# Layer 0's B rows by broadcast transfers instead of bf16 split and select matmuls, and a second PSUM bank for the preparation

## The reference

```python
x_dbl = u @ w_xproj
delta = softplus(x_dbl[..., :DT_RANK] @ w_dt + b_dt)
Bm, Cm = x_dbl[..., DT_RANK:DT_RANK+16], x_dbl[..., DT_RANK+16:]
def step(h, inp):                       # over the 256 tokens
    d_t, b_t, c_t, u_t = inp
    dA = exp(d_t[..., None] * A)
    h = dA * h + (d_t * u_t)[..., None] * b_t[:, None, :]
    return h, einsum('bdn,bn->bd', h, c_t)
```

## Time and profile before

| | |
|---|---|
| median of runs | 2923.34 us |
| profiled execution | 2917.5 us, its span 2916.2 us |
| layer 0 (load to the end of its last sum) | to about 985 us of the span |
| full turns (t = 2 to 14) | 53.3 us each |
| of a full turn's 53 us | PE busy 47.27, DVE 49.44, ACT 28.60, POOL 23.03 us |
| granted TensorE clock | mean 0.945 over the span |

### The profile page before, as it was taken

One profiled execution on the slowest core, in us unless ns is written; L12 is line 12 of the kernel. 1 busy time (PEld: TensorE's weight loads), 2 busy tenths in 40 slices (PEclk: granted clock), 3 DMA queues, 4 the chain that ended last, 5 costly groups with the idle time before them and its releaser, 6 DMA issues.

```text
span 2916.2 us, 47757 instructions
## 1 busy us (share of the span) xinstructions
PE 2373.6 (81%) x18201; PEld 1678.6 (58%) x18201; DVE 2152.4 (74%) x4587; ACT 1433.4 (49%) x3688; POOL 839.7 (29%) x453
## 2 busy tenths in 40 slices
PE   4788889889887757888888888858999976676776
PEld 2456666666665654666666666635666654454544
DVE  3389999999988443767676767645666626999997
ACT  0355555555555114676767676613434334555553
POOL 0044344344444301222222222200000002555444
PEclk9999999999998877999999999969999998999988
DMA  1011110111111450000000000010110003445442
GB/s 63 16 38 38 45 45 30 45 45 41 42 37 52 148 180 1 1 1 2 1 2 1 1 1 1 1 38 20 29 29 8 6 25 117 159 146 167 145 169 95
DMA packets 71348, 147.97 MB, mean 51 GB/s; under 512 B 6864, under 2 KB 37072, under 8 KB 70608
## 3 DMA queue, kind: packets, MB, share of 16 engines
q1 hardware_dynamic: 69072, 140.73, 14.5%
q0 software_dynamic: 2048, 4.20, 0.4%
HBM read 135.20 MB, written 9.18 MB: 50 GB/s over the span
## 4 chain that ended last, share of the span: by engine, by line
PE 48%; DVE 21%; issue 12%; POOL 9%; ACT 7%; DMA 2%; SPq 0%; POOLq 0%; DVEq 0%; ACTq 0%
POOL h L2125 6%; PE psum L831 4%; PE psum L651 4%; DVE mx L1392 4%; DVE h L1514 3%; PE psum L647 3%; PE psum L389 2%; PE psum L699 2%; PE psum L538 2%; ACT pt L1880 2%; DVE h L1505 2%; PE psum L658 2%; PE psum L583 2%; PE psum L780 2%; PE psum L416 2%
## 5 line engine op out<-in xcount | busy, mean ns | idle before, releaser
L2091 POOL TENSOR_TENSOR h<-h,Crep 128x1024 f32<-128x1024 f32 x128 | 371.6, 2915 | 609.2 <-DVE h L1514 609.2
L2073 POOL TENSOR_TENSOR pr<-pr,rsum 128x512 f32<-128x512 f32 x192 | 202.2, 1057 | 643.9 <-DVE rsum L1358 642.2
L1514 DVE TENSOR_TENSOR_SCAN h<-dA,h 128x1024 f32<-128x1024 f32 x128 | 292.1, 2304 | 3.9 <-DVE h L1505 0.5
L1392 DVE TENSOR_REDUCE mx<-psum 128x4 f32<-128x1024 f32 (+1 forms) x192 | 226.5, 1215 | 80.0 <-PE psum L656 80.0
L2125 POOL TENSOR_TENSOR h<-h,Crep 128x1024 f32<-128x1024 f32 x64 | 196.4, 3068 | 243.3 <-DVE h L1268 243.3
L1880 ACT ACTIVATE pt<-psum 128x1024 f32<-128x1024 f32 x192 | 186.9, 1017 | 128.0 <-PE psum L658 128.0
L831 PE MATMUL psum<-h,pack_wf 128*128 128x256 f32 x1024 | 243.1, 392 | 5.4 <-POOL h L2091 5.4
L831 PEld LDWEIGHTS psum<-h,pack_wf 128*128 128x128 f32 x1024 | 199.9, 199 | 34.7 <-POOL h L2091 6.4
L1836 ACT ACTIVATE pr<-psum,nb 128x256 f32<-128x256 f32 (+1 forms) x512 | 210.5, 432 | 15.8 <-DVE nb L1350 15.8
L1977 ACT ACTIVATE dA<-delta,A 128x255 f32<-128x255 f32 x512 | 211.4, 495 | 13.1 <-DVE h L1514 11.7
L1846 ACT ACTIVATE prT<-psum 128x512 f32<-128x512 f32 x192 | 115.7, 603 | 163.1 <-PE psum L552 162.4
(11 more groups left out here) (342 smaller groups left out, 5426.9 us busy)
## 6 DMA issues: line engine op xcount, KB each, us to landing
Crep<-c_rows SPq DMA_DIRECT2D x64, 512.0 KB, 3.9
Brep<-bc_rows SPq DMA_DIRECT2D x64, 512.0 KB, 6.5
Crep<-bc_rows SPq DMA_DIRECT2D x64, 512.0 KB, 5.9
w1r<-m_w SPq DMA_DIRECT2D x32, 256.0 KB, 5.8
w2r<-m_w SPq DMA_DIRECT2D x32, 256.0 KB, 5.5
pack_wf<-wf SPq DMA_DIRECT2D x1, 3192.0 KB, 12.5
slots<-zero SPq DMA_DIRECT2D x12, 256.0 KB, 3.0
w1s<-s_w SPq DMA_DIRECT2D x8, 256.0 KB, 2.8
```

The lines of the kernel that those rows point to most:

```text
L1392: ve.e.tensor_reduce(mx[:, qb, 2 * h:2 * h + 2, groups[0]:groups[-1] + 1], k.psum[:, base:base + 2, :].rearrange("p i (n x) -> p i n x", n ...
L1514: ve.e.tensor_tensor_scan(flat(h), flat(k.dA[c][g % 2]), flat(h), 0.0, ALU.mult, ALU.add).then_inc(*k.set("scanned", 0, b, g, c))
L2091: po.e.tensor_tensor(h[:, :, :], h[:, :, :], k.Crep[n % 3][:, :, :], ALU.mult).then_inc(*k.set("hC", 0, b, g, c))
```

## The change

B takes the way that C had. `crow` (32 rows, B and C) is stored whole to DRAM, and `sp_b_spread` reads four B rows back, repeated for all partitions, into one of two Brep tiles in SBUF. The product reads Brep there, whole groups at a time (128x1024, one instruction for each c), and the scan of c waits for its own product alone. The bf16 split on DVE, the select matmuls on PE, the `selb` matrix and its cast are gone; empty steps stand in the table where the split was. Bank 6, which held the spread rows, becomes the second bank of the preparation: its steps alternate between banks 5 and 6, with a wait of their own where the single bank had implied one. The SP queue carries 64 more transfers of 512 KB.

```diff
+def pe_take0(k, s):
+
+    if k.pre0_read[s] is not None:
+        k.pe.wait_ge(*k.at(*k.pre0_read[s]))
+    return k.bank[s]
...
     yield
-    bk = pe_take(k, 0)
+    bk = pe_take0(k, 6)
+    pe.wait_ge(*k.at("xnT", 0, b))
     pe.e.matmul(bk[0:E0, 0:L], w["gate_w"], xnT[:, :], start=True, stop=True).then_inc(*k.set("gate", b))
-    k.pre_read = ("gz", b)
+    k.pre0_read[6] = ("gz", b)
     yield
-    bk = pe_take(k, 0)
+    bk = pe_take0(k, 5)
...
-        pe.e.matmul(bk[0:96, 0:L], w["w_bc"][:, c, :], u[:, c, :], start=c == 0, stop=c == CI - 1)
+        pe.e.matmul(bk[0:32, 0:L], w["w_bc"][:, c, :], u[:, c, :], start=c == 0, stop=c == CI - 1)
...
-def pe_spread(k, b, g, j):
...
-        i = pe.e.matmul(SB[:, m * L:(m + 1) * L], w["sel"][:, g * NG + 2 * j + m, :], k.split[b % 2][:, :], start=True, stop=True)
...
-    ve.e.tensor_copy(k.crow[b % 2][:, :], bk[0:32, 0:L]).then_inc(*k.set("crow", b))
-    yield
-    if b >= 2:
-        ve.wait_ge(*k.at("spread", 0, b - 2, 3, "B", 1))
-    ve.e.tensor_copy(split[:, :], bk[0:96, 0:L]).then_inc(*ve.step())
-    yield from rest(ve)
-    ve.e.tensor_tensor(k.sr[:, :], bk[0:64, 0:L], split[0:64, :], ALU.subtract).then_inc(*k.set("bc_read", b))
-    yield
-    ve.wait_ge(*k.at("bc_read", b))
-    ve.e.tensor_copy(split[0:64, :], k.sr[:, :]).then_inc(*ve.step())
-    yield from rest(ve)
-    ve.e.tensor_tensor(split[0:32, :], k.sr[0:32, :], split[0:32, :], ALU.subtract).then_inc(*k.set("split", 0, b))
+    ve.e.tensor_copy(k.crow[b % 2][:, :], b6[0:32, 0:L]).then_inc(*k.set("crow", b))
+    yield
+    yield
+    yield
+    yield
...
-def ve_product(k, b, g, j):
-    ve, SB = k.ve, k.bank[SPREAD_BANK]
+def ve_product(k, b, g, c):
+    ve, n = k.ve, 4 * b + g
     was = (b, g - 2) if g >= 2 else (b - 1, g + 2) if b else None
     ve.wait_ge(*k.at("dtu", b))
-    ve.wait_ge(*k.at("spread", 0, b, g, "B", j))
-    for c in range(CI):
-        if was is not None:
-            ve.wait_ge(*k.at("summed", 0, *was, c))
-        i = ve.e.tensor_tensor(k.h[c][g % 2][:, 2 * j:2 * j + 2, :], bcast(k.dtu[b % 2][:, c, :], 2, 1),
-                               SB[:, :].rearrange("p (n t) -> p n t", n=2), ALU.mult)
-    i.then_inc(*k.set("dbu", 0, b, g, j))
+    ve.wait_ge(*k.at(f"b_spread{n % 2}", "L0", b, g))
+    if was is not None:
+        ve.wait_ge(*k.at("summed", 0, *was, c))
+    ve.e.tensor_tensor(k.h[c][g % 2][:, :, :], bcast(k.dtu[b % 2][:, c, :], NG, 1), k.Brep[n % 2][:, :, :],
+                       ALU.mult).then_inc(*k.set("dbu", 0, b, g, c))
...
-    ve.wait_ge(*k.at("dbu", 0, b, g, 1))
+    ve.wait_ge(*k.at("dbu", 0, b, g, c))
...
+def sp_b_spread(k, b, g):
+
+    sp, n = k.sp, 4 * b + g
+    if not 0 <= b < NB:
+        return
+    sp.wait_ge(*k.at(f"c_stored{b % 2}", b))
+    if n >= 2:
+        sp.wait_ge(*k.at("dbu", 0, (n - 2) // 4, (n - 2) % 4, CI - 1))
+    rows = bcast(k.bc_rows[b % 2, g * NG:(g + 1) * NG, :], P, 0)
+    sp.e.dma_start(k.Brep[n % 2][:, :, :], rows).then_inc(*k.set(f"b_spread{n % 2}", "L0", b, g, by=16))
...
     for t in range(NB + 2):
+        sp_b_spread(k, t - 2, 2)
         if 0 <= t - 2 < NB:
             sp_c_spread(k, t - 2, 3)
+        sp_b_spread(k, t - 2, 3)
         if 0 <= t - 1 < NB:
             sp_c_store(k, t - 1)
             sp_c_spread(k, t - 1, 0)
+        sp_b_spread(k, t - 1, 0)
+        if 0 <= t - 1 < NB:
             sp_c_spread(k, t - 1, 1)
         if t + 1 < NB:
             sp_negmax(k, 0, t + 1)
+        sp_b_spread(k, t - 1, 1)
         if 0 <= t - 1 < NB:
             sp_c_spread(k, t - 1, 2)
...
-    ve.e.tensor_copy(k.sel[:, :, :], bcast(w["sel"], P, 2))
-    w["sel"] = k.sel[:, :, :]
```

More of the change, by code:

```diff
@@ L102 @@
     "x_ve": ("x1", "x1_sum", "x_attn", "x_mamba", "x_ffn", "x_spread", "x_moe", "x_ssm", "x_gathered"),
-    "mamba_ve": ("sx", "split", "zin", "delta", "dtu", "dtT", "bc_read", "u", "y_read", "yT", "st_norm", "lT"),
+    "mamba_ve": ("sx", "zin", "delta", "dtu", "dtT", "bc_read", "u", "y_read", "yT", "st_norm", "lT"),
     "moe_ve": ("hs_up", "hs"),
@@ L353, in pe_pre0 @@
     i.then_inc(*k.set("merged_mm", b))
-    k.pre_read = ("merged", b)
+    k.pre0_read[6] = ("merged", b)
     yield
-    bk = pe_take(k, 0)
+    bk = pe_take0(k, 5)
     pe.e.matmul(bk[:, 0:L], w["wk0"][:, 0, :], xnT[:, :], start=True, stop=True)
@@ L795, in pe_inner @@
     i.then_inc(*k.set("bc", 0, b))
-    k.pre_read = ("bc_read", b)
+    k.pre0_read[6] = ("crow", b)
     yield
-    bk = pe_take(k, 0)
+    bk = pe_take0(k, 5)
+    pe.wait_ge(*k.at("crow", b))
     for c in range(CI):
@@ L801, in pe_inner @@
     i.then_inc(*k.set("dt", 0, b))
-    k.pre_read = ("zin", 0, b)
-SPREADS = ((1, 1), (2, 0), (2, 1), (3, 0), (3, 1), (4, 0), (4, 1), (5, 0))
-def pe_spread(k, b, g, j):
-    pe, w, SB = k.pe, k.w, k.bank[SPREAD_BANK]
-    pe.wait_ge(*k.at("split", 0, b))
-    was = (b, g, 0) if j else (b, g - 1, 1) if g else (b - 1, 3, 1) if b else None
-    if was is not None:
-        pe.wait_ge(*k.at("dbu", 0, *was))
-    for m in range(2):
-        i = pe.e.matmul(SB[:, m * L:(m + 1) * L], w["sel"][:, g * NG + 2 * j + m, :], k.split[b % 2][:, :], start=True, stop=True)
-    i.then_inc(*k.set("spread", 0, b, g, "B", j))
+    k.pre0_read[5] = ("zin", 0, b)
 def pe_sums(k, b, g):
@@ L1025, in ve_pre0 @@
 def ve_pre0(k, b):
-    ve, bk, w = k.ve, k.bank[PRE_BANK[0]], k.w
+    ve, bk, b6, w = k.ve, k.bank[5], k.bank[6], k.w
     yield from ve_norm(k, 0, b)
@@ L1058, in ve_pre0 @@
     ve.wait_ge(*k.at("merged_mm", b))
-    ve.e.tensor_copy(k.merged[:, :, b], bk[:, 0:E0]).then_inc(*k.set("merged", b))
+    ve.e.tensor_copy(k.merged[:, :, b], b6[:, 0:E0]).then_inc(*k.set("merged", b))
     yield
@@ L1444, in ve_inner @@
 def ve_inner(k, b):
-    ve, bk, w = k.ve, k.bank[PRE_BANK[0]], k.w
-    split, su = k.split[b % 2], k.su[b % 2]
+    ve, bk, b6, w, su = k.ve, k.bank[5], k.bank[6], k.w, k.su[b % 2]
     yield
@@ L2297, in place_mamba @@
     k.delta, k.dtu = k.two("delta", [P, CI, L]), k.two("dtu", [P, CI, L])
-    k.split, k.crow, k.sr = k.two("split", [96, L], BF16), k.two("crow", [32, L]), k.sb("sr", [64, L])
+    k.crow = k.two("crow", [32, L])
     k.dA, k.h = [k.two("dA", [P, NG, L]) for c in range(CI)], [k.two("h", [P, NG, L]) for c in range(CI)]
-    k.Crep = k.two("Crep", [P, NG, L], n=3)
+    k.Crep, k.Brep = k.two("Crep", [P, NG, L], n=3), k.two("Brep", [P, NG, L])
     k.A = k.sb("A", [P, CI, NS])
@@ L2374, in load, with turn0 @@
         phase_end(k, q, "load")
-def turn0(k, t, e, pre, out, wide, inner, states, results, summing=None):
+def turn0(k, t, e, pre, out, wide, inner, states, results):
     merge(ORDER[0],
           (results(k, t - 3), e + "_results") if results is not None and 0 <= t - 3 < NB else None,
-          (states(k, t - 2), e + "_states") if -1 <= t - 2 <= NB else None,
-          (summing(k, t - 2), e + "_summing") if summing is not None and -1 <= t - 2 <= NB else None,
+          (states(k, t - 2), ("pe_summing" if e == "pe" else e + "_states")) if -1 <= t - 2 <= NB else None,
           (out(k, 0, t - 1), e + "_out") if 0 <= t - 1 < NB else None,
```

52 lines of the change are left out of this document (23 added, 29 removed).

## The result

The changed kernel takes 2942.6 us (median of 4 runs, 2938.2 to 2947.4) where the kernel before took 2923.2 beside it: a ratio of 1.0068, 95% interval 1.0049 to 1.0087. It is slower by some 20 us, which is what was forecast (2943). The profiled execution of after has a span of 2936.9 us, against 2916.2.

A forecast was written before the change was run, and what follows sets the result against it. DVE and PE are nearly full in layer 0 (49.44 and 47.27 of 53 us). -10.3 ahead, +25.4 in 13 full turns and +4.5 in the last three give +19.6: 2943 us, range 2930 to 2960, wide range 2902 to 2972.

The forecast's parts named there:

- The hold: DVE's products, now reading two SBUF tiles, stand still until POOL's multiplication is done: 4.75 us a full turn.
- the waiting engine goes next: When DVE and POOL both ask for two SBUF tiles, the one that has waited goes next; first hold 2.1 us.
- product first: Rival: DVE's next product takes the port though POOL waits; a turn costs about +0.5 us, total 2923; 17%.
- The saving: On DVE, split gone, longer products, shorter scan waits: -2.2 us a turn.
- free products: Rival: holds do not come or idle time swallows them; some -2.0 us a turn, about 2886 us; 16%.
- The full turns: Turns 2 to 14: holds less savings and idle time give +1.95 us each, +25.4 over 13.
- Transfers: B transfers on the queue: group 1's alone costs some 0.6 us a turn, counted as nothing; bounds 0 to 0.6.
- Ahead of the full turns: Two preparations' bank waits 5.5, selb cast 2.2 and turns 0 and 1 2.6 us go: -10.3 us.
- The first max of turn 0: Sign to look for: the first max in turn 0 comes about 7.7 us sooner.
- Behind the full turns: Last three turns, where DVE's list is shorter: 1.5 us each, +4.5 us.
- The clock: PE's granted clock in full turns: below 1.00 was named a sign that the forecast is wrong.
- The rival's mechanism: Rival: PE's clock falls around 575 to 590 in every turn; some 2 us more a turn, 2970 us; 14%.

The follow-up runs named there:

- 1: Kernel before, only the products' second operand made a constant SBUF tile instead of the PSUM bank; ratio 1.0491 to the kernel before.
- 3: Changed kernel with POOL's multiplication cut to the first four columns of each row; ratio 0.9851 to the kernel before.
- 2: Kernel before with POOL's multiplication cut to the first four columns of each row; ratio 0.9955 to the uncut kernel before.
- 8: Changed kernel with B transferred only for the first two groups, the other 62 transfers left out; ratio 1.0089 to the kernel before.
- 7: Changed kernel with bank 5 alone for a batch's preparation, bank 6 unused; ratio 1.0139 to the kernel before.
- 5: Changed kernel with three DVE products moved to other places in the turn; ratio 1.0016 to the kernel before, median 2919 us.
- 9: Changed kernel with ten filler matmuls (results unread) ahead of L721's second half on PE; ratio 1.0114 to the kernel before.
- 10: Changed kernel with three DVE products moved and eleven filler matmuls instead of five ahead of yT on PE; ratio 0.9958 to the kernel before.
- 4: Changed kernel with one product (group 1, c = 0) moved from behind the second scan to behind the sum of x; ratio 1.0041 to the kernel before.

## Why the prediction was right, step by step

**The hold** was forecast at 4.75 us a turn and measured 4.9. Its parts: 2.1 forecast and 2.12 measured; 0.35 and 0.03; 0.6 and 0.72; 0.5 and 0.69; 1.2 and 1.38. That the waiting engine goes next held in after (531.39 is one multiplication long, not two) and again in 1. The rule of the Trainium skill, "SBUF — State Buffer", section "Who interferes with whom", that two SBUF inputs make a DVE instruction contend with GpSimd and one does not, agrees with 1: the same product takes 1.28 us a pair from PSUM and up to 5.52 from SBUF. The rival *product first* fell with it.

**The saving** on DVE, 2.2 us a turn, is what its busy time shows in 3 against 2 (49.75 to 47.57). In the length of the turn 3 against 2 gives only 1.1, where the rival *free products* had 2.0; a B wait of 1.1 us instead of 0.6 is in it. That rival (2886, or 36 us less) described 3 roughly, with 31 us less than 2, and not after.

**The full turns** came to +27.3 where +25.4 was forecast. A turn of 55.2 is 1.9 us longer than before, as forecast: busy time 2.3 us up, idle time 0.4 us down, where the forecast had 2.55 and 0.6.

**Transfers** were counted at nothing because the hold covers them: right, by 8.

**Ahead of the full turns** -10.3 was forecast and -17.0 measured. This is the term that was mis-sized. The prediction took away the 5.5 us of waits in the two preparations; 7 shows that with the bank the last matmuls of each preparation also take little more than half the time, and that all but about 1 us of the 17.0 is the bank's: 10.4 in the preparations, for which 5.5 stood in the sum, and 5.7 in turns 0 and 1, for which there were 1.2. The first max of turn 0 came 13.7 us sooner (57.94 and 44.28) and not 7.7. The saved cast of 2.2 is in the 1 that is left, with something in turns 0 and 1 against it.

**Behind the full turns** +4.5 was forecast and +10.4 measured. The last turns have longer holds, since two products stand back to back against POOL's pairs:

```profile
904.76 4.49 DVE L1481 TENSOR_TENSOR h<-dtu,Brep 128x1024 f32<-128x1024 f32 x2
...
986.58 6.58 DVE L1481 TENSOR_TENSOR h<-dtu,Brep 128x1024 f32<-128x1024 f32 x2
```

With the short hC the same part differs by 1.7 us, so some 9 of the 10.4 come from POOL's multiplications. The two misses, -6.7 and +5.9, nearly cancel, and with the +1.9 of the full turns the span grew by 20.7 us where 19.6 was forecast; that the sum came out this close is in part luck.

**The clock.** The forecast kept it at 1.00 in full turns and named a lower one as a sign against it; it fell to 0.91 to 0.97 in every one of them, where before only the first and the last stood below 1.00 (0.94 and 0.95). PE was busy 46.7 us and not some 45: L824 alone took 5.3 us instead of 3.6 at the lower level. Its wait for yT, for which 1 us more was forecast, is the 1.07 us of before. The rival's mechanism was there and its price was not: it had 2 us a turn, and it was 1.6 us in one turn and nothing that shows in the ten of 55.2. The forecast held in spite of it, because DVE is held at the place where the clock mostly falls; it had not reckoned with that. The Trainium skill, "TensorE: Matmul & The Clock Gate", section "HAM oscillation — how this bites in real kernels", describes waits between bursts that bring the slow level back. There the waits are for DMA; here they are for DVE, 1.82 us in 5 and 2.36 in 9, and the fall stands behind them, in 5 in some turns only. Where PE is on the chain it costs 1.6 us a turn (5, 10).

## What to carry to other kernels

Moving an operand of a DVE instruction from PSUM to SBUF can make it collide with GpSimd: price it by what POOL has pending at that place, at most one of POOL's instructions for each DVE instruction, and so prefer few long ones. A hold or wait that is taken away shows the next chain at once; read who is late behind it, and which other instruction now comes at a bad moment, before the gain is booked (4). And a stretch of slow clock costs by where it stands: keeping PE busy pays at a wait on the chain (10), and can be worse than nothing elsewhere (9).
